# Four bias buffers, a new order of the sync queue's loads, later results in small slots, and one 128-row slot moved to the middle

## What is computed

```python
xn = _layernorm(x)
g, v, d = xn @ Wg + bg, xn @ Wv + bv, xn @ Wd + bd
scan = linear_scan(sigmoid(g) * tanh(v), 0.001 + 0.998 * sigmoid(d))
scores = sigmoid(xf @ Wg.T + bg + bias)            # 4096 tokens x 8 experts
top_scores, top_idx = top_k(scores, 2)
h = gelu(einsum('td,ehd->teh', xf, W1) + b1)       # H = 1024
eo = einsum('teh,edh->ted', h, W2) + b2
combined = einsum('ted,te->td', eo, weights)       # weights: the two scores, else 0
shared = gelu(xf @ Ws1.T + bs1) @ Ws2.T + bs2
out = x + scan + shared + combined
```

## Time and profile before

| | us |
|---|---|
| median of 3 executions | 699.54 (699.03 to 699.96) |
| the profiled execution | 703.41 |
| its span, first to last instruction | 701.6 |
| PE busy | 647.4 (92%) |
| DVE busy | 512.4 (73%) |
| ACT busy | 435.6 (62%) |
| POOL busy | 281.5 (40%) |

### The profile page before, as it was taken

The page is one execution under the profiler, slowest core; times in us unless marked ns, Lnnn a source line. Parts: engine busy times, 40 slices in busy tenths (PEclk is TensorE's granted clock), DMA queues, the critical chain, the costliest instruction groups (busy, mean ns, idle before and its releaser), DMA issues.

```text
span 701.6 us, 19821 instructions
## 1 busy us (share of the span) xinstructions
PE 647.4 (92%) x6246; PEld 509.4 (73%) x6247; DVE 512.4 (73%) x1328; ACT 435.6 (62%) x774; POOL 281.5 (40%) x263
## 2 busy tenths in 40 slices
PE   4899999999999998999999999997989798988984
PEld 3475756666675756888888988886878687877873
DVE  4899899999999889776666666664656556665663
ACT  6988696969687674455555555654555454545562
POOL 2133242424242454354464544452535344444323
PEclk9999999999999999999999999999999989999998
DMA  7534436262433242243332446455564636464653
GB/s 245 186 76 136 121 92 159 82 179 63 147 90 120 62 120 55 77 70 54 61 63 54 71 101 144 85 123 166 114 175 118 183 81 171 108 169 110 178 155 39
DMA packets 63264, 80.77 MB, mean 115 GB/s; under 512 B 19492, under 2 KB 55268, under 8 KB 60376
## 3 DMA queue, kind: packets, MB, share of 16 engines
q1 hardware_dynamic: 48072, 62.08, 28.5%
q0 software_dynamic: 15120, 17.77, 15.8%
HBM read 38.66 MB, written 18.10 MB: 81 GB/s over the span
## 4 chain that ended last, share of the span: by engine, by line
PE 35%; issue 23%; DMA 17%; POOL 11%; DVE 7%; ACT 4%; SPq 3%; POOLq 0%; DVEq 0%; ACTq 0%
PE bank L1351 12%; PE bank L1343 12%; DMA out<-arena,slot_adds 11%; POOL out L570 8%; PE bank L1331 6%; DMA b2row<-in_b 3%; POOL rows L557 2%; ACT arena L656 1%; POOL arena L557 1%; DVE arena L963 1%; DVE W L866 1%; PE bank L1322 1%; DVE arena L962 1%; SPq L383 1%; PE bank L1404 1%
## 5 line engine op out<-in xcount | busy, mean ns | idle before, releaser
L1343 PE MATMUL bank<-rows,W 128*128 128x256 f16 (+1 forms) x1728 | 276.9, 300 | 4.0 <-issue 2.3
L1351 PE MATMUL bank<-W,arena 128*128 (+1 forms) x2112 | 276.7, 273 | 4.1 <-DVE arena L963 3.8
L1351 PEld LDWEIGHTS bank<-W,arena 128*128 128x128 f16 x2112 | 202.0, 98 | 39.2 <-issue 4.4
L656 ACT ACTIVATE arena<-bank,par 128x256 f32<-128x256 f32 (+2 forms) x344 | 165.4, 516 | 98.3 <-PE bank L1343 90.8
L1343 PEld LDWEIGHTS bank<-rows,W 128*128 (+1 forms) x1728 | 166.8, 99 | 58.7 <-issue 6.2
L570 POOL DMA_INDIRECT out<-arena,slot_adds x71 | 116.6, 1642 | 211.5 <-ACT arena L781 169.0
L962 DVE TENSOR_SCALAR arena<-arena,par 128x256 f16<-128x256 f32 (+1 forms) x284 | 101.3, 357 | 58.2 <-ACT arena L656 56.9
L963 DVE SCALAR_TENSOR_TENSOR arena<-arena,par 128x256 f16<-128x256 f32 (+1 forms) x284 | 133.9, 471 | 10.0
L514 POOL DMA_INDIRECT lists<-entry,place x64 | 70.6, 1104 | 124.6 <-ACT arena L638 66.5
L1331 PE MATMUL bank<-rows,W 128*128 128x512 f16 x288 | 63.8, 379 | 0.0
L662 ACT ACTIVATE rows<-bank 128x1024 f16<-128x1024 f16 (+2 forms) x43 | 36.2, 842 | 35.1 <-PE bank L1423 33.3
(11 more groups left out here) (187 smaller groups left out, 602.6 us busy)
## 6 DMA issues: line engine op xcount, KB each, us to landing
stage<-in_w SPq DMA_DIRECT2D x32, 512.0 KB, 5.1
stage<-W SPq DMA_DIRECT2D x15, 1024.0 KB, 5.2
arena<-W SPq DMA_DIRECT2D x7, 1024.0 KB, 4.7
b2row<-in_b SPq DMA_DIRECT2D x43, 128.0 KB, 3.3
arena<-in_x SPq DMA_DIRECT2D x8, 512.0 KB, 5.3
xhl_rows<-W SPq DMA_DIRECT2D x8, 512.0 KB, 4.4
out<-arena SPq DMA_DIRECT2D x8, 512.0 KB, 6.0
W<-in_w SPq DMA_DIRECT2D x4, 512.0 KB, 9.1
```

Of the source, the lines that this page charges most:

```text
L656: ins = A(h32[k][:, c], ps_e[k][:, c], ACT.Gelu, bias=p[:, 4 + e * i + jj:5 + e * i + jj], scale=p[:, 0:1])
L1343: ins = T.matmul(bank_, weights(w, wp * HALF + c * H + j * P, P), rhs[:, 2 * xp + c, :], start=n == 0, stop=n == 3 * KD - 1)
L1351: ins = T.matmul(banks[t // 2][:, (t % 2) * D:(t % 2 + 1) * D], h[:, hp, t * P:(t + 1) * P], weights(w, (2 + wp) * HALF + j * D, D), start ...
```

## The change

It has four parts.

1. **Bias rows four deep.** `b2rows` has the two old buffers and two in `arena[4096:4608]`. SP now loads the bias row of **n + 2** in the step of n, when the result of n - 2 has been made (`bias_of`). For n = 0 and 1 it waits until the last base rows are stored, since they lay where the new buffers are.
2. **SP's order.** In a step come first the row list of n + 4 and the bias of n + 2, then the copies for small slots, and at the end the wait for the addition of n - 2 with the list of adds of n + 2. The copies also start earlier: those for the next LOW slot one and two slots behind a LOW slot, the one for the next MID slot one slot behind a MID slot.
3. **DVE in small slots.** `result` of the slot before stands behind the split of unit 1 and `parameters` behind that of unit 2.
4. **Order of slots.** The lone MID slot goes from the end to n = 14, between the 14 ROWS slots and the seven trips. The program now ends with a trip: ROWS, LOW, ROWS, MID. `last_w1_in` is gone, since every MID slot takes its copy from `mid_w1`.

```diff
-FIRST, TRIPS = NA // 2, NA // 4
-TRIP = (ROWS, LOW, ROWS, MID)
+FIRST = NA // 2
+SIZES = (ROWS,) * FIRST + (MID,) + (ROWS, LOW, ROWS, MID) * NC
...
+        b2rows = [b2row[0], b2row[1], arena[:, 4096:4096 + D], arena[:, 4096 + D:4096 + 2 * D]]
...
-            def step(s, s2, s4):
-
-                if s4 is not None:
-                    sp.wait_ge(rows_in[s.c], s.got)
-                    load_list(s4, slot_rows, rows_list_in)
-                if not isinstance(s.n, int) or s.n >= 2:
-                    sp.wait_ge(y_ok, s.n + S_A + 1)
-                    second_bias(s)
-                if s2 is not None:
-                    if not isinstance(s.n, int) or s.n >= 2:
-                        sp.wait_ge(add_out[s.u], s.added - 16 * s.tiles)
-                    load_list(s2, slot_adds, adds_list_in)
+            def rows_list(s, s4):
+                sp.wait_ge(rows_in[s.c], s.got)
+                load_list(s4, slot_rows, rows_list_in)
+
+            def bias_of(s, s2):
+
+                if s.n < 2:
+                    sp.wait_ge(o_out, 16 * SEQS)
+                else:
+                    sp.wait_ge(y_ok, s.n + S_A + 1)
+                second_bias(s2)
+
+            def adds_list(s, s2):
+                if s.n >= 2:
+                    sp.wait_ge(add_out[s.u], s.added - 16 * s.tiles)
+                load_list(s2, slot_adds, adds_list_in)
...
-                    sp.wait_ge(y_ps, s.unit - TRIP_UNITS + s.units + H_A + RING)
+                    sp.wait_ge(y_ps, used.unit + used.units + H_A + RING)
...
-                    sp.wait_ge(ev_ps, s.unit - TRIP_UNITS + s.units + EV_A)
+                    sp.wait_ge(ev_ps, used.unit + used.units + EV_A)
...
+            for n in range(SLOTS):
+                s = order(n)
+                if n == FIRST - 4:
+                    sp.wait_ge(route_ok, 2)
+                if n + 4 < SLOTS:
+                    rows_list(s, order(n + 4))
+                if n + 2 < SLOTS:
+                    bias_of(s, order(n + 2))
                 if n == FIRST - 3:
-                    sp.wait_ge(route_ok, 2)
...
+                    mid_weights(mids[0], None)
+                for l in range(2):
+                    if n == FIRST - 2 + l:
+                        low_weights(lows[0], l, None)
+                for k in range(1, NC):
+                    for l in range(2):
+                        if n == lows[k - 1].n + 1 + l:
+                            low_weights(lows[k], l, lows[k - 1])
+                for k in range(1, NB):
+                    if n == mids[k - 1].n + 1:
+                        mid_weights(mids[k], mids[k - 1])
+                if n + 2 < SLOTS:
+                    adds_list(s, order(n + 2))
...
             def small_slot(s, back, nxt):
 
                 for k in range(s.units):
                     split_h(s, k)
-                    if k == 0:
+                    if k == 1:
                         result(back)
-                        if nxt is not None:
-                            dve.wait_ge(y_ok, back.n + S_A + 1 + 2)
-                            parameters(nxt)
...
+                    if k == 2 and nxt is not None:
+                        dve.wait_ge(y_ok, back.n + S_A + 1 + 2)
+                        parameters(nxt)
```

More of the change, by code:

```diff
@@ L63 @@
 UNITS = {ROWS: KH, MID: KH // 2, LOW: KH // 2}
-TRIP_UNITS = sum(UNITS[r] for r in TRIP)
+COLUMN = {ROWS: 0, MID: NA, LOW: NA + NB}
+assert [SIZES.count(r) for r in (ROWS, MID, LOW)] == [NA, NB, NC]
 PER = 45
@@ L72, with __init__ @@
 class Slot:
-    def __init__(self, n, c, rows, column, unit, got, added):
-        self.n, self.c, self.rows, self.column, self.unit = n, c % DEEP, rows, column, unit
-        self.got, self.added = got, added
+    def __init__(self, n, c, rows, kth, unit, got, added, smaller=None):
+        self.n, self.c, self.rows, self.kth, self.unit = n, c % DEEP, rows, kth, unit
+        self.got, self.added, self.smaller = got, added, smaller
+        self.column = kth + COLUMN[rows]
         self.u, self.units = c % 2, UNITS[rows]
         self.tiles, self.parts = max(rows // P, 1), min(rows, P)
-        self.weighed = None if rows == ROWS else (column - NA - NB) * 2 + 1 if rows == LOW else (column - NA) * 2 + 2
 def ahead(n, c):
     return Slot(n, c, ROWS, n, n * KH, (n - c % DEEP) * 8 + 32, (n - c % 2) * 16 + 32)
[L88 to L97, removed]
-def order(n):
[L102 to L108, removed]
+def order(n):
+    if not 0 <= n < SLOTS:
+        return None
+    past = SIZES[:n]
+    dmas = [16 * max(r // P, 1) for r in SIZES[:n + 1]]
+    return Slot(n, n, SIZES[n], past.count(SIZES[n]), sum(UNITS[r] for r in past), sum(dmas[n % DEEP::DEEP]),
+                sum(dmas[n % 2::2]), sum(r < ROWS for r in past))
 class Tally:
@@ L1270, in _ @@
             slot(order(FIRST - 1), order(FIRST - 2), order(FIRST))
-            for t in range(TRIPS):
-                one_trip(t)
-            small_slot(order(SLOTS - 1), order(SLOTS - 2), None)
+            for n in range(FIRST, SLOTS):
+                (slot if SIZES[n] == ROWS else small_slot)(order(n), order(n - 1), order(n + 1))
             result(order(SLOTS - 1))
@@ L1539, in _ @@
                          turn2=order(n + 2) if n == FIRST - 1 else None)
[L1540 to L1542 removed]
+            for n in range(FIRST, SLOTS):
+                w = slot(order(n), order(n + 1), w, turn2=order(n + 2),
+                         back=order(n - 1) if SIZES[n - 1] == LOW else None)
 def kernel(**inputs):
```

108 lines of the change are left out of this document (29 added, 79 removed).

## The result

The changed kernel takes 679.75 us in the median (678.43 to 680.72), the kernel before on the same chip 699.75 (699.03 to 700.64). The ratio is 0.971, with a 95% interval of 0.969 to 0.974. It is faster by 20.0 us; the forecast was 31.0, and the time lies 0.75 us above the range. The profiled execution took 678.43 us, with a span of 676.6.

A forecast was written before the change was run, and what follows sets the result against it. PE was taken to set the pace to about 447 us, then late biases and splits in small slots. 0.61 + 31.85 + 5.5 - 5.7 = 32.3, less 1.3 for small waits, gives 31.0 off: 668.5 us, range 665 to 673 (0.76).

The forecast's parts named there:

- The late bias: Small slots: bias load issued behind SP's unrelated wait for an addition; issued early, all 46.5 us of ACT's waits go.
- The clean trip of 31.00 us: PE's trip without waits, summed from clean pieces: 31.00 us against 36.31, so six trips lose 31.85.
- The share given to the clock: PE in the trips: of 31.85 us lost, waits account for some 22.5; the rest, 9 us, is mostly half clock.
- The addition chain: A trip's additions, each landing before the next is issued, take 26.1 us against 31.0: 4.9 us of room.
- the rival in which all additions are slow: Additions sharing DMA engines with copies take 7.14 us each: trip 35.4, result 693.5; 0.08 for sharing in part or whole.
- DVE's order: Small slots: `result` and `parameters` behind later splits lets the second split come in time, 1.1 us to spare.
- the first rival: DVE still holds small slots: each of 15 keeps 0.61 us of split wait, 9.2 us, about 677; chance 0.12.
- the fourth unit of LOW slots: The tight place: DVE's fourth split in LOW slots has from +0.4 to -0.1 us left before PE wants it.
- nothing is near: MID slots: a unit of PE takes 1.33 us and not 1.0, so no split there was expected to be tight.
- The tail and the moved slot: Lone MID slot moved: end falls from 19.8 to 14.3 us, gaining 5.5; the middle takes 5.7; together nothing.
- SP's copies, costed at nothing: Earlier copies on SP remove PE's 4.0 us of waits; the list of adds queued behind has some 15 us cover.
- The offset: Median taken as 3.87 us below the profiled execution: 672.4 profiled becomes 668.5.

The follow-up runs named there:

- its four groups: The changed kernel, unaltered, measured four times beside the kernel before: 679.75, 681.85, 673.90 and 680.11 us.
- With the LOW copies behind: Changed kernel with only the 64-row slots' copies put behind SP's wait for an addition and list of adds: 670.95 us, later 676.14 us.
- the first trace: Profile of the changed kernel's first measurement, nothing altered: median 679.75 us, profiled execution 678.43 us, span 676.6.
- the fourth group: One chip: changed kernel again 673.90 us; LOW copies behind SP's wait 670.95; MID copies behind 674.13; list of adds before copies, lone MID slot last 676.85.
- 680.66 both times: Changed kernel with MID slots' first layer read straight from `W`, lone MID slot in the middle, then last: 680.66 us each.
- the second group: One chip: changed kernel again 681.85 us; parameters four deep 681.70; also later in ROWS slots 681.64; small slots' copies left out except first of each 673.38.
- the fifth group: A further chip: changed kernel again 680.11 us; with the LOW slots' copies behind SP's wait and list of adds 676.14 us.
- the first and the fourth: The first: changed kernel with DVE's old order 687.19 us, bias two deep 716.12, lone MID last 679.81; kernel before with DVE's new order 713.85.
- the third: Changed kernel with SP's wait and list ahead of copies 672.33 us; then MID from `W` 680.66; all small slots from `W` 700.43; MID from `W`, lone last 680.66.
- the quiet one: Trace of the unaltered changed kernel where PE had no unnamed stop: median 673.90 us, span 672.0.
- the best version: Changed kernel with the LOW slots' copies behind SP's wait for an addition and list of adds: 670.95 us, ratio 0.958.

## Why the prediction was right and wrong

**The late bias, right.** The wait had to do with where SP issued the load. Early, it is gone; put back alone, the wait is 45.2 us again, and the time is 34 to 42 us above the changed kernel's in its four groups.

**The clean trip of 31.00 us, right.** With the LOW copies behind, six trips take 30.93 each at a clock of 1.00. The share given to the clock was right too: the windows of the kernel before with a granted clock under 1.00 (0.91, 0.97, 0.86 and 0.91, between 480 and 640 us) come to 20 x 0.35 = 7.0 us, of the 9 that the waits left. The addition chain (26.1 us by the prediction) does not bind: no `result` waits for a landing in that trace, and PE is busy for 199.87 of the 200 us from 440 to 640. So the rival in which all additions are slow did not come true, though the additions do land later beside copies.

**DVE's order, right in size, wrong in place.** Without it PE waits 0.6 us in each small slot, as the first rival had it, so that the rival's condition is met only when the order is undone. With it PE's waits in small slots are 1.9 us, under the 2 forecast. But they don't stand at the fourth unit of LOW slots: the first trace has four of the five in MID slots, where by the prediction "nothing is near", the largest (0.83) in the last. The other tight place, which the prediction did not look at, is the ROWS slot behind a LOW slot, at unit 4, where `parameters` for the MID slot come: 0.9 us of PE's waits in the first trace and 2.4 in the fourth group's. Its reading of DVE's idle time before `parameters`, up to 0.76, was also short: it is up to 1.1 in the first trace and 1.4 in the fourth group's.

**The tail and the moved slot, right.** The tail took 13.8 us for 14.3, and the place of the lone slot is worth nothing where no copy is in the way (680.66 both times). What the sum didn't hold: with the one MID buffer, a lone slot at the end would wait 5 us for its copy.

**SP's copies, costed at nothing: the step that failed.** The prediction asked what is queued behind the copy on SP, found 15 us of cover, and stopped there; it considered the copy's DMA traffic only against the additions. The copy hits a third party: DVE, which waits for no data of it. Its load of a register takes 0.30 us without copies and up to 1.12 when a copy has gone out 0.9 to 3 us before. Having the LOW copies so early costs 673.90 - 670.95 = 2.95 us in one group and 4.0 in another. Less those 2.95 the first result would have been 676.8, inside the range. That the copies slow the loads is shown; that the loads make all of the 3 us is not, since PE's waits for splits make 2.4 of 3.7 us of span, and in the second group a shorter stop of DVE gave nothing.

**What no step held: stops without a name.** The changed kernel took 673.90 us on one chip and 679.75, 681.85 and 680.11 elsewhere, and the kernel before 699.3 to 700.2 beside all of them. The difference is 6 to 8 us. With it come stops of PE, ACT and DVE which the profile lays to `issue` or `remote`. They don't make up all of it: PE's are 1.1, 3.1 and 2.3 us in three traces whose spans are 4.6, 7.4 and 6.3 us longer than the quiet one's 672.0. What is shown: they follow the group and not the version. In the second and the fifth group each version with copies has 2.3 to 3.2 us of PE's, and in the first and the fourth no version of the changed kernel has any; the third is in between, with none where the copies stay and 0.8 to 4.2 us in the versions that read `W` at a register. In the second group they went when the copies were left out, and in the fifth PE's stayed when the LOW copies were moved behind the wait. They don't follow the loads of instructions, of which the quiet trace has as many. Here are the instruction queues between 440 and 660 us, of the changed kernel's first trace and of the quiet one:

```profile
q8 instruction: 24, 0.39, 0.8%
q14 instruction: 13, 0.11, 0.1%
```
```profile
q8 instruction: 25, 0.41, 0.8%
q14 instruction: 14, 0.11, 0.2%
```

What makes them, and why some chips have none, stays open. Each group ran on one chip and at one time, so that the chip itself is the cause is not shown either.

**The offset.** I took the profiled execution to lie 3.87 us above the median, as in the run of before. After the change it lay 1.3 below, as the lowest of four. Executions of the kernel before are several us apart (697.1 to 704.0 in one group), so nothing showed this difference to be constant, and it should have stood in the range, not in the sum. Of the 11.2 us missed, 5.2 are this.

Put together by medians: from the forecast of 668.5 to the best version's 670.95 it is 2.45 us, in which the offset and a better span (668.3 for the 670.6 forecast) partly cancel; the LOW copies add 2.95, and what comes with the unnamed stops the other 5.85 of the first result.

## What to carry to other kernels

When a large transfer is moved, ask not only who waits for it and who is queued behind it, but what runs in the few us after its issue, even if it shares no data: here the load of a register by an engine without slack. An edit can gain beside another and lose by itself: late `result` gains where the bias is early, and alone it loses 1.6%. And take a profiled execution's distance from the median as noise of the size of the runs' spread, not as a constant.

## What the runs showed of the hardware

While a copy of 1 MB within SBUF runs, DVE's load of a register takes up to 1.12 us (fourth group), against 0.298 to 0.317 for all 28 without copies, and its stop before the tile addressed by that register grows from 0.26 to 1.08 us in the same slot. PE's loads grow too, to 0.91 us at most with the LOW copies behind. I had not expected this, since DVE reads nothing that the copy writes.

The same program in groups of runs on different chips differed by 6 to 8 us in 680, while the kernel before was the same within 1 us. That small stops show only in a kernel whose PE is nearly full, and hide in the waits of a slacker one, is a possible reading that no run tests.

Reading 64-row matrix operands at a register's offset instead of from a copy at a fixed place cost 19.8 us more than doing so for MID slots alone (700.43 against 680.66). The same 288 products of the second layer kept PE busy for 25.0 us instead of 12.3.
